# A transformer layer with routed experts on one core: the work around the table stage reordered, and the last tiles' norm put ahead of experts' low parts

## The reference

```
dA   = (1 + dtA/2) / (1 - dtA/2)                    # one complex number z for each of 256 x 64 (h, n)
K    = 2 * Re( sum_n Ct[c,h,n] * z[h,n] ** l )      # l = 0 .. 511: tokens (8, 256, 512)
h    = concat([cls_tok, K], axis=1)                 # (8, 257, 512)
h    = h + Attention(layernorm(h))                  # 16 heads; q and k scaled by cos and sin of a rotation
x    = layernorm(h)
p,i  = top_2(softmax(x @ router_w + router_b))      # 8 experts
h    = h + (sum_k p_k * gelu(x @ expert_w[i_k] + expert_b[i_k])) @ out_w + out_b
```

## Time and profile before

| | us |
|---|---|
| median of three runs | 748.42 (747.17 to 749.06) |
| the profiled execution | 749.32 |
| its span, first to last instruction | 747.6 |
| PE busy | 679.0 (91%) |
| DVE busy | 526.1 (70%) |
| ACT busy | 413.2 (55%) |
| POOL busy | 151.3 (20%) |

### The profile page before, as it was taken

The page is one execution under the profiler, slowest core; times in us unless marked ns, Lnnn a source line. Parts: engine busy times, 40 slices in busy tenths (PEclk is TensorE's granted clock), DMA queues, the critical chain, the costliest instruction groups (busy, mean ns, idle before and its releaser), DMA issues.

```text
span 747.6 us, 16676 instructions
## 1 busy us (share of the span) xinstructions
PE 679.0 (91%) x5671; PEld 543.2 (73%) x5672; DVE 526.1 (70%) x1211; ACT 413.2 (55%) x1071; POOL 151.3 (20%) x306
## 2 busy tenths in 40 slices
PE   4688887879999999999999999888769999998998
PEld 4477877867778787777878777656448888886786
DVE  7988993556778777787877876678774444445775
ACT  4865544476667677676766766575623333333111
POOL 5200001010121111202112120113032333326560
PEclk9899999989999999999999999999779999999999
DMA  7500356400000010000100004125716765656894
GB/s 208 189 2 15 128 114 147 97 1 1 3 21 37 0 53 3 28 28 14 42 0 28 28 28 145 54 74 208 254 56 195 205 203 169 168 166 203 258 324 175
DMA packets 54553, 76.11 MB, mean 102 GB/s; under 512 B 24666, under 2 KB 26970, under 8 KB 54387
## 3 DMA queue, kind: packets, MB, share of 16 engines
q1 hardware_dynamic: 40850, 42.43, 17.6%
q0 software_dynamic: 5920, 19.40, 9.9%
q10 hardware_dynamic: 7744, 13.77, 5.0%
HBM read 45.42 MB, written 30.16 MB: 101 GB/s over the span
## 4 chain that ended last, share of the span: by engine, by line
PE 74%; DVE 13%; ACT 6%; DMA 3%; issue 2%; POOL 1%; ACTq 0%; DVEq 0%; POOLq 0%
PE ps L1969 45%; PE ps L2072 9%; PE ps L2082 4%; PE ps L2065 4%; PE ps L2133 4%; DVE ring L1401 3%; DVE ring L1402 3%; PE ps L1916 2%; DMA wo_raw<-in_L_attn_Wo_dram 2%; PE ps L2089 1%; ACT prb L1021 1%; DVE ew_lo L1713 1%; ACT pts L1029 1%; PE ps L2032 1%; PE ps L1960 1%
## 5 line engine op out<-in xcount | busy, mean ns | idle before, releaser
L1029 ACT ACTIVATE pts<-ps 128x512 f32<-128x512 f32 x128 | 77.1, 602 | 97.5 <-PE ps L2072 97.4
L1021 ACT ACTIVATE prb<-ps,negmax 128x257 f32<-128x257 f32 x256 | 117.7, 478 | 4.7 <-DVE negmax L1472 3.7
L1472 DVE TENSOR_REDUCE negmax<-ps 128x2 f32<-128x514 f32 x128 | 82.5, 686 | 21.4 <-PE ps L2065 21.4
L2072 PE MATMUL ps<-ident,prb 128*128 128x128 f32 x512 | 83.9, 288 | 6.2 <-ACT pts L1029 3.2
L2072 PEld LDWEIGHTS ps<-ident,prb 128*128 128x128 f32 x512 | 57.3, 144 | 30.7 <-issue 12.0
L1481 DVE TENSOR_SCALAR prb<-prb,rrec 128x258 f32<-128x258 f32 x256 | 73.4, 351 | 2.3
L1203 ACT ACTIVATE rows<-ps 128x512 f32<-128x512 f32 x40 | 23.9, 598 | 84.7 <-DVE ps L1826 82.7
L1969 PE MATMUL ps<-ew_hi,xnT_hi 128*128 x160 | 67.0, 419 | 0.1
L1969 PE MATMUL ps<-ew_lo,xnT_hi 128*128 x160 | 63.4, 396 | 0.0
L1969 PE MATMUL ps<-ew_hi,xnT_lo 128*128 x160 | 63.1, 394 | 0.0
L1746 DVE TENSOR_TENSOR xnT_lo<-ps,xnT_hi 128x512 fp32r<-128x512 f32 x40 | 27.7, 691 | 49.6 <-ACT xnT_hi L1163 31.1
(11 more groups left out here) (402 smaller groups left out, 1772.5 us busy)
## 6 DMA issues: line engine op xcount, KB each, us to landing
y_slots<-rows ACTq DMA_DIRECT2D x40, 256.0 KB
ew<-in_L_ffn_expert_w_dram SPq DMA_DIRECT2D x8, 1024.0 KB, 9.0
h_dram<-h_ob SPq DMA_DIRECT2D x17, 256.0 KB, 2.0
xn_dram<-tok SPq DMA_DIRECT2D x17, 256.0 KB, 2.2
h_late<-h_dram SPq DMA_DIRECT2D x12, 256.0 KB
out_dram<-h_late SPq DMA_DIRECT2D x11, 256.0 KB
y_slots<-u_sb SPq DMA_DIRECT2D x9, 256.0 KB, 5.8
tok_dram<-so SPq DMA_DIRECT2D x4, 512.0 KB, 3.2
```

The source lines that it names most:

```text
L1021: e = act.activation(prb[:, u % 2, j, 0:KEYS], ps[:, j, 0:KEYS], ACT.Exp, bias=negmax[:, u % 2, j:j + 1], accum_out=rowsum[:, u % 2, j:j + 1])
L1029: act.activation(pts[:, slot:slot + 2, :, st * P:(st + 1) * P], ps[:, 4, :].rearrange("p (h t s) -> p h t s", h=2, t=HALVES), ACT.Copy).th ...
L1472: dve.tensor_reduce(negmax[:, u % 2, 2 * b:2 * b + 2], ps[:, 2 * b:2 * b + 2, 0:KEYS], AX_X, ALU.max, negate=True).then_inc(s["dve_max"], 1)
L2072: mm = pe.transpose(ps[:, 4, (2 * j + tt) * P:(2 * j + tt + 1) * P], prb[:, u % 2, 2 * b + j, tt * P:(tt + 1) * P], ident[:, :])
```

## The change

At startup:

- The copies of `zs` to `zt` for the first six powers go from DVE to ACT, between the low part of Wv and the high part of Wo; DVE waits for them.
- PE turns `r_low` right behind the class row's value, ahead of Wq; piece 0 between turning Wq and subtracting its high part; piece 1 between Wq and Wk; the other pieces follow Wk. ACT has the same order. `W_BANK` of Wk becomes 4 to 7, so that banks 0 to 3 are the tables'; `W_AFTER` says which matrix's low part must have been copied from a bank.
- `low_powers(1)` uses the scratch of `ring` 0 instead of `ring` 1 and waits for the piece before the last.
- ACT keeps the four low banks of half 1 before tokens 2 and 3, and the first piece of half 1 between these two.
- DVE copies the class column to `xT_lo` behind the first norm instead of ahead of it.

From attention to the experts:

- ACT copies `oT`'s last high part ahead of expert 0's; expert 2's high part moves behind the next four turned tiles, expert 3's behind the last logits.
- DVE: residual and statistics of tile 0 come ahead of all low parts, then half of expert 0's, then tile 1, the sums, the other half, and the last tiles' norm, which is now ahead of the class rows. Expert 1's low part follows the class rows' statistics. Expert 2's goes behind the routing.
- DVE computes `token_of` right behind the one-hot matrices, ahead of `slot_of` and `expert_of`.

```diff
-    W_BANK = (4, 0, 4, 0)
+    W_BANK = (4, 0, 4, 4)
+    W_AFTER = {2: 0, 3: 2}
+    TABLE_POWERS_DONE = 3 * 5
...
             w_low(0, wvT_lo)
+            act.wait_ge(s["dve_power_step"], TABLE_POWERS_DONE)
+            act.activation(zt[:, 0:NZ - 1, :, 0, :], zs[:, 0:NZ - 1, :, 1, :], ACT.Copy, scale=-1.0).then_inc(s["act_params"], 1)
+            act.activation(zt[:, 0:NZ - 1, :, 1, :], zs[:, 0:NZ - 1, :, 0, :], ACT.Copy).then_inc(s["act_params"], 1)
             w_high(1, woT_hi)
...
             for q in range(LOW_TURNS):
                 turned(q, rT, 4 * q)
-            keep_pieces(0, 0, 2)
+            w_scale(wk_raw, k_scale)
+            w_high(2, wqT_hi)
+            keep_pieces(0, 0, 1)
+            w_low(2, wqT_lo)
+            act.activation(bvc_hi[:, :], bv_col[:, :], ACT.Copy).then_inc(s["act_bias_high"], 1)
+            keep_pieces(0, 1, 2)
+            w_high(3, wkT_hi)
+            w_low(3, wkT_lo)
...
             keep_pieces(0, 2, PIECES)
-            keep_tokens(0, 1, 2, 3)
+            keep_tokens(0, 1)
             for q in range(LOW_TURNS):
                 turned(TURNS + q, rT, 4 * q)
-            keep_pieces(1, 0, upper + GROUP)
+            keep_tokens(2)
+            keep_pieces(1, 0, 1)
+            keep_tokens(3)
+            keep_pieces(1, 1, upper + GROUP)
...
+            hi_ot(last, 3)
             hi_expert(0)
-            hi_ot(last, 3)
             hi_expert(1)
             act.wait_ge(s["pe_pv"], NB * KC)
-            hi_expert(2)
...
                 if q == EARLY_QUADS:
-                    hi_expert(3)
+                    hi_expert(2)
                 keep_lgT(q)
+            hi_expert(3)
             hi_expert(4)
...
-            swapped(zt[:, 0:NZ - 1], zs[:, 0:NZ - 1])
-            settle()
+            dve.wait_ge(s["act_params"], 4)
...
                 if hf == 1:
-                    dve.wait_ge(s["pe_table_turned"], max(turned_before(1, p) for p in (1, upper + 2)))
+                    dve.wait_ge(s["pe_table_turned"], max(turned_before(1, p) for p in (0, upper + 2)))
...
-                    tmp = ring[:, 1, 0, 0:n]
+                    tmp = ring[:, 1 - hf, 0, 0:n]
...
-            dve.wait_ge(s["act_xT_high"], 1)
-            dve.tensor_copy(xT_lo[:, :, BODY:KPAD], xc_lo[:, :, :].bitcast(F32)).then_inc(s["dve_xT_low"], 1)
             dve.memset(lnr[:, :, :], 1.0).then_inc(s["dve_spread"], 1)
...
             ln_apply(0, (0, NB), P)
+            dve.wait_ge(s["act_xT_high"], 1)
+            dve.tensor_copy(xT_lo[:, :, BODY:KPAD], xc_lo[:, :, :].bitcast(F32)).then_inc(s["dve_xT_low"], 1)
...
+            def lo_chunks(e, k0, k1):
+                dve.wait_ge(s["act_expert_high"], e + 1)
+                return dve.tensor_tensor(ew_lo[:, e, k0:k1, :], ew[:, e, k0:k1, :], ew_hi[:, e, k0:k1, :].bitcast(F32),
+                                         ALU.subtract)
...
             top_two(1)
-            for e in range(2):
-                lo_expert(e)
             residual(last, 0, 6)
             dve.wait_ge(s["dve_residual"], last * HALVES + 1)
             residual_stats(last, 0)
-            lo_expert(2)
+            lo_chunks(0, 0, KC // 2)
             residual(last, 1, 7)
             dve.wait_ge(s["dve_residual"], last * HALVES + 2)
             residual_stats(last, 1)
             dve.wait_ge(s["dve_stats2"], 5 * last + 2)
             norm_sums(last)
+            lo_chunks(0, KC // 2, KC).then_inc(s["dve_expert_low"], 1)
+            for st in range(HALVES):
+                normalise(last, st)
...
-            for st in range(HALVES):
-                normalise(last, st)
+            lo_expert(1)
             dve.wait_ge(s["pool_rstd"], NB + 1)
...
+            dve.wait_ge(s["pe_token_of"], 1)
+            then(dve.tensor_copy(token_tile[:, :], ps[:, 2, 0:SLOTS]))
+            dve.scalar_tensor_tensor(out=token_of[:, :], in0=token_tile[:, :], scalar=float(P),
+                                     in1=ps[:, 2, SLOTS:2 * SLOTS], op0=ALU.mult, op1=ALU.add
+                                     ).then_inc(s["dve_token_of"], 1)
...
+            lo_expert(2)
+            lo_chunks(LOWS_IN_ATTENTION + 1, KC // 2, KC)
+            lo_chunks(LOWS_IN_ATTENTION + 2, 0, KC)
...
+            pe.wait_ge(s["act_w_low"], 2 * KC)
+            turn_low(0)
             pe.wait_ge(s["act_w_scaled"], KC)
             w_turn(wq_raw, 2)
+            turn_pieces(0, 0, 1)
             w_rest(wqT_hi, 2)
+            turn_pieces(0, 1, 2)
             pe.wait_ge(s["act_w_scaled"], 2 * KC)
             w_turn(wk_raw, 3)
             w_rest(wkT_hi, 3)
+            turn_pieces(0, 2, PIECES)
             pe.wait_ge(s["act_w_low"], 4 * KC)
-            turn_low(0)
-            turn_pieces(0, 0, PIECES)
             tokens_of_half()
```

More of the change, by code:

```diff
@@ L983, in _ @@
                 turned(q, rT, 4 * q)
-            keep_pieces(0, 0, 2)
+            act.wait_ge(s["loaded_wk"], 16)
+            act.wait_ge(s["pool_angles"], 4)
+            w_scale(wk_raw, k_scale)
[6 more added lines that the diff above has]
+            w_low(3, wkT_lo)
+            act.wait_ge(s["act_bias_high"], 1)
+            act.activation(bvc_neg[:, :], bvc_hi[:, :].bitcast(F32), ACT.Copy, scale=-1.0).then_inc(s["act_bias_high"], 1)
             act.wait_ge(s["dve_power_step"], CHANNELS_DONE)
@@ L1339, in channel_powers @@
                 link(dve.tensor_tensor(g_im, t0, inv, ALU.mult))
-                dve.wait_ge(s["act_params"], 5)
+                dve.wait_ge(s["act_params"], 7)
                 for lv in range(3):
@@ L1802, in _ @@
             dve.tensor_scalar(stores_used[:, :], pairs_used[:, 1:2], 16.0, None, ALU.mult).then_inc(s["dve_stores_used"], 1)
-            dve.wait_ge(s["pe_token_of"], 1)
-            then(dve.tensor_copy(token_tile[:, :], ps[:, 2, 0:SLOTS]))
-            dve.scalar_tensor_tensor(out=token_of[:, :], in0=token_tile[:, :], scalar=float(P),
-                                     in1=ps[:, 2, SLOTS:2 * SLOTS], op0=ALU.mult, op1=ALU.add
-                                     ).then_inc(s["dve_token_of"], 1)
             dve.wait_ge(s["act_route_exp"], 1)
```

26 lines of the change are left out of this document (5 added, 21 removed).

## The result

The changed kernel takes 743.08 us (median of 6 runs, 740.77 to 745.11) against 748.16 for the kernel before (6 runs, 746.10 to 749.37): ratio 0.9940, interval 0.9914 to 0.9966, 5.1 us or 0.6% faster where 739.5 was forecast. Its profiled execution took 743.96 with a span of 742.2.

The account below looks back on a forecast made before the run. PE, busy nine tenths of the span, bounds the kernel, so only its waits can shrink. Startup 4.5 + passage 4.2 + token order 0.4 = 9.1 us off the 748.42 median, stated as 739.5; own range 738.5 to 741, 8-in-10 range 736.5 to 743.

Parts of the forecast that it names:

- the stall of DVE at the third piece: Startup, first half: DVE's 2.34 us wait until 44.90 goes; with 1.07 the half ends 3.4 us earlier.
- at 43.8 to 45.8: Startup, first half: when PE, done with Wk's rest at 43, would turn piece 2.
- The rival that had the startup held by ACT and PE, 742: Startup: late copies of piece 2 stall DVE again, 2.6 us less gain, 742 us; chance 0.20.
- The swap on ACT: Startup powers: two DVE copies go to ACT, so DVE's next operation starts 1.07 us earlier.
- The second half: Startup tables: DVE restarts at 83.3 instead of 87.46, 4.2 us earlier in all, 0.8 of it gained here.
- The first norm: End of startup: norm ahead of the class column's copy gains nothing up to 1.7 us; 0.3 counted.
- Passage up to the chain: Attention's end to the routing chain: chain starts 4.2 us earlier (3.6 to 4.4), the class rows setting the end.
- POOL was shut out, and that rival has fallen: Class rows: rival said POOL is not shut out by DVE, passage gives 6.0, 737.6 us; chance 0.22.
- the clock should hold: Passage, last tiles' norm: PE's 2.42 us wait goes, so its clock stays up.
- Token order: `token_of` ahead of the slot chain: first gather 0.9 us earlier, 0.4 left at the experts' first product.
- The first two gathers took 1.39 and 0.96 us; that rival has fallen: Experts' gathers: rival said DVE's low parts shut them out, experts start 3.5 us later, 743 us; chance 0.08.
- The sum: Whole kernel: startup 4.5, passage 4.2 and token order 0.4 make 9.1 us; median 739.5 us forecast.

Follow-up runs that it names:

- passage alone: Only the edits from attention's end to the experts, startup as in the kernel before: 743.44 us, 0.9948 of the kernel before.
- startup padded later: Only the startup's edits, plus two extra DVE memsets behind the second half's last piece: 746.43 us, 0.9974 of the kernel before.
- filled: Changed kernel plus 20 idle PE turns ahead of the first half's third piece: 739.93 us, 0.9906 of the kernel before.
- slots first: Changed kernel with the first two slot tiles' low parts ahead of expert 5's: 742.84 us, 0.9940 of the kernel before.
- the changed kernel's third: Changed kernel again, unedited, third set of runs: 742.72 us, 0.9933 of the kernel before.
- the parts alone: Each half of the diff alone against the kernel before: passage 0.9948; startup 1.0031 and, repeated, 1.0024.
- without the gap: Startup's edits alone plus two extra DVE memsets, at the powers (744.87 us, 0.9971) or behind the second half's last piece (746.43 us, 0.9974).
- the bias first: Changed kernel with POOL adding the class rows' bias ahead of their power: 739.50 us, 0.9916 of the kernel before.

## Why the prediction was wrong

**The step that failed** is the one on the stall of DVE at the third piece: "the stall of 2.34 goes", and "the first half ends 1.07 + 2.34 = 3.4 us earlier." The piece did start 3.35 us earlier, but the half ended only 2.31 earlier. First, the stall was no fixed property of the order before. In its first profile a late start of `r_low` (2.37 us) and its slow turn (1.66 us) met; the second profile has no stall, and the first scores of before lay at 136.18, 133.97 and (passage alone) 137.65. Second, the sum let PE turn piece 2 "at 43.8 to 45.8", at full clock. It started at 43.97, but behind a pause of its own, and the three pieces took 7.19 us: the clock was low, as in nine of thirteen profiles, and a stall of 0.84 to 2.08 stood two pieces on. The rival that had the startup held by ACT and PE, 742, comes nearest; it had the stall come back by late copies on ACT, and it came back by PE's clock. The mean of the first scores is 135.9 over those three and 133.4 over the thirteen: 2.5 us, where 4.5 were forecast. Where neither stalls nor finds the clock low after 120 us (133.97 against 132.09, 131.98 and 132.29) it is 1.9.

**Startup, the other terms.** The swap on ACT: 1.06 of 1.07. The second half: the restart came 3.27 earlier in place of 4.2, 0.9 missing where the first half was 1.1 short; the wait of 2.41 us was foreseen as 2.4. The first norm: PE turned it 3.50 earlier, 0.23 more than the restart, where 0.3 was counted. But in all thirteen profiles with the new order on PE it stands idle 0.20 to 0.64 us without a releaser behind the second product of the second tokens (0.50 at 123.72), where both profiles of before, and the passage alone, have no such gap. From the norm to the first scores it takes 14.4 to 14.9 us in place of 14.16 in both profiles of before, where the clock stays up. No term of the sum held that.

**Passage up to the chain.** Right in mechanism: POOL was shut out, and that rival has fallen. The size, 4.42 where 4.2 was forecast, repeated as 4.6, is in part the clock's. At a high clock it is 23.3 us (startup padded later) against 21.3 to 21.6, some 1.9; at a low one 26.0 against 22.7 (filled, slots first; 0.88 and 0.89), 3.3. The prediction's "the clock should hold" came true in part: in the changed kernel's first two profiles the clock fell 2.5 and 1.4 us ahead of the chain's start, in these two some 5 us ahead of it.

**Token order.** 0.63 at the first product where 0.4 was forecast; but the sixth tile came 42.40 us behind the start of the chain before and 42.18 after, in the second profiles 42.45 and 42.34, and 43.13 in the changed kernel's third: nothing of this term is shown to last. The first two gathers took 1.39 and 0.96 us; that rival has fallen.

**Attention.** The sum held its time constant. Over all profiles it lies between 366.5 and 370.4 us, for either kernel; one pair of profiles can therefore show 2.2 us that belong to neither. On average the changed kernel has no more low clock than before: its mean granted clock over the whole span is 0.970, 0.973 and 0.971 in three sets of runs, that of before 0.969 to 0.972 in five.

**The sum.** Startup 2.5, passage 4.4 and 0.2 make 7.1 us by stages; the three comparisons give 4.5 to 5.1, each with an interval of some 1.6 either way, and the parts alone 0.9948 and, without the gap, 0.9971 and 0.9974, which make 6 us. Some 1 to 2.6 us between stages and medians stay unexplained; one cause may be that the low stretch of the old passage is absent in some executions, as in one of the four profiles with its order and no gap, but no run measures how often. Last, the base was high: the profiled execution of before had both its startup stall and 749.32 us, while the later medians of before were 746.89 to 747.85.

## What to carry to other kernels

- Before a stall is counted as gain, look at the granted clock beneath it, and take a second profile: a wait behind a matmul group that takes twice its usual time belongs at least in part to the clock and may be elsewhere in the next execution. Here the second profile of the kernel before, taken ahead of the prediction, would have shown no stall.
- An engine that runs ahead stands idle later. On PE that pause may not be free: in nine of thirteen profiles the low clock began within it or just behind it. Filling it with 20 idle turns went with a full clock and no stall of DVE in one profile; a gain in time is shown only for that and the bias first together (0.9878 against 0.9933).
- An edit can cost time far away, in code that it leaves alone, by moving what follows in an engine's program. If a part alone is slower without a reason in its own stretch, look for idle time without a releaser and pad by the instructions removed.

## What the runs showed of the hardware

- A gap of 0.27 us on DVE came and went with two instructions more or fewer in its program (two profiles with it, two padded ones without), and cost 2 us since POOL then got the shared ports first. On PE the new order brought a gap of 0.5 us behind the second of 128 products; with 20 more instructions ahead it stood behind the 110th in both profiles, at 1.87 and 1.95 us. That is 108 products on, or 128 less the 20 that were added. No run varied it on purpose; the place in the program fits both.
- The lock works both ways: POOL's power of two columns takes 0.69 to 0.93 us with no two-input product of DVE beside it and 2.66 with one; DVE's half product of 1.21 us took 1.80 behind POOL's bias; and a norm of DVE with one input from SBUF, 0.55 us, took 1.85 behind it. The Trainium skill, "SBUF — State Buffer", section "Who interferes with whom", says that `tensor_scalar` too can run in a mode that takes the shared pair, and that whichever engine starts first keeps it for its whole instruction; the rows agree.
- A short low stretch can be passed on and grow. With the clock at 0.70 in place of 1.00 at 14 to 18 us, ACT's `sines` came 1.57 us later, POOL then met DVE's long products, and the scaling of Wq that waits for POOL came 3.11 us later.
- PE's idle of 2.4 us ahead of the last tiles' turns was followed by a low clock in three profiles (eight turns in 1.91 to 1.97 us) and by a high one in a fourth (1.11).
- The same unedited kernel shows single runs from 741.3 to 752.2 us; the longer ones have the lower mean granted clock (0.977 for the first, 0.964 for the last).
